# Addressing the V product's weight slices through TensorE registers loaded from a table

## The reference

```
src_trans = jnp.einsum('bsf,of->bso', src, W_src) + b_src      # src: (8, 512, 512), W_src: (512, 512)
src_key, src_val = jnp.split(src_trans, 2, axis=2)             # K: outputs 0 to 255, V: outputs 256 to 511
...
attn = jax.nn.softmax(scores, axis=-1)
tgt_update = jnp.einsum('bhts,bshd->bthd', attn, v)
```

## Time and profile before

| | |
|---|---|
| time, median of 2 runs | 1054.62 us (1053.51 to 1055.73) |
| time of the profiled execution | 1049.61 us |
| its span, first to last instruction | 1047.5 us |
| PE busy | 1003.0 us (96%) |
| PEld busy | 761.4 us (73%) |
| DVE, ACT, POOL busy | 655.4, 467.2, 389.4 us |
| mean granted TensorE clock | 0.989 of full speed |

### The profile page before, as it was taken

How to read it: one execution, slowest core, us unless ns; L and a number is a source line. 1 busy time by engine, 2 the same in 40 slices (tenths; PEclk the granted TensorE clock), 3 DMA queues, 4 the chain that set the end, 5 groups by cost and what they waited for, 6 DMA issues and landing times.

```text
span 1047.5 us, 14744 instructions
## 1 busy us (share of the span) xinstructions
PE 1003.0 (96%) x5070; PEld 761.4 (73%) x5070; DVE 655.4 (63%) x1510; ACT 467.2 (45%) x881; POOL 389.4 (37%) x355
## 2 busy tenths in 40 slices
PE   4889999999999998899999999999999999999998
PEld 3656767676767664567888888888888888888886
DVE  6866767776767577445665566556556556555544
ACT  3447565666565646445424333333333333333322
POOL 2569797879797967345310010010010100100000
PEclk9999999999999997999999999999999999999999
DMA  7543342424242223325333232242341232332230
GB/s 232 131 132 93 101 132 67 128 72 134 70 114 70 65 64 101 81 81 122 95 72 68 52 81 58 54 82 50 63 80 42 71 82 46 74 75 60 67 72 24
DMA packets 84377, 87.87 MB, mean 84 GB/s; under 512 B 13160, under 2 KB 66296, under 8 KB 84304
## 3 DMA queue, kind: packets, MB, share of 16 engines
q1 hardware_dynamic: 82384, 84.85, 32.9%
q10 hardware_dynamic: 1920, 2.10, 0.6%
HBM read 56.99 MB, written 4.46 MB: 59 GB/s over the span
## 4 chain that ended last, share of the span: by engine, by line
PE 89%; DVE 5%; ACT 2%; SPq 1%; issue 1%; POOL 1%; DMA 1%; DVEq 0%; ACTq 0%; POOLq 0%
PE ps L659 49%; PE pst L659 18%; PE ps L765 5%; PE ps L738 5%; PE pst L754 5%; PE ps L665 4%; DVE mx L1196 1%; PE ps L778 1%; SPq L611 1%; SPq L546 1%; ACT e_buf L866 1%; DVE lg L1277 1%; ACT ctx_h L866 0%; DVE wsrc_l L1145 0%; DMA x<-in_x 0%
## 5 line engine op out<-in xcount | busy, mean ns | idle before, releaser
L659 PE MATMUL ps<-x_h,weights 128*128 128x512 f32 x1088 | 365.6, 397 | 2.8 <-DVE sg L1297 2.0
L659 PEld LDWEIGHTS ps<-x_h,weights 128*128 128x128 f32 x1088 | 204.4, 188 | 52.7 <-issue 2.5
L1196 DVE TENSOR_REDUCE mx<-ps 128x1 f32<-128x512 f32 x256 | 173.2, 684 | 95.4 <-PE ps L738 94.8
L659 PE MATMUL ps<-x_l,weights 128*128 128x512 f32 x544 | 214.5, 394 | 0.0
L866 ACT ACTIVATE hh<-qb 128x512 fp32r<-128x512 f32 x136 | 86.0, 632 | 287.7 <-DVE qb L1311 268.2
L659 PE MATMUL pst<-hh,weights 128*128 128x512 f32 x544 | 193.2, 397 | 0.0
L866 ACT ACTIVATE e_buf<-pst 128x512 f32<-128x512 f32 x256 | 147.1, 595 | 100.4 <-PE pst L754 90.5
L1300 DVE TENSOR_TENSOR qb<-ps,sg 128x512 f32<-128x512 f32 x136 | 94.0, 691 | 135.9 <-PE ps L659 132.2
L1316 DVE TENSOR_TENSOR hl<-qb,hh 128x512 fp32r<-128x512 f32 x136 | 94.3, 693 | 92.2 <-ACT hh L866 92.0
L1406 POOL TENSOR_TENSOR e_sums<-e_sums,e_buf 128x1024 f32<-128x1024 f32 x60 | 143.4, 2390 | 8.6 <-ACT e_buf L866 2.5
L1358 POOL TENSOR_SCALAR ve<-mv 128x4 f32<-128x4 f32 x8 | 1.8, 229 | 337.8 <-DVE mv L1238 337.8
(11 more groups left out here) (154 smaller groups left out, 1360.7 us busy)
## 6 DMA issues: line engine op xcount, KB each, us to landing
cb<-combine_scratch SPq DMA_DIRECT2D x128, 256.0 KB, 4.7
q_stack<-q_h SPq DMA_DIRECT2D x128, 64.0 KB, 2.0
k_stack<-k_h SPq DMA_DIRECT2D x124, 64.0 KB, 2.0
ctx_raw<-in_ctxT SPq DMA_DIRECT2D x7, 1024.0 KB, 5.3
q_stack<-q_l SPq DMA_DIRECT2D x64, 64.0 KB, 2.0
out_x<-ob SPq DMA_DIRECT2D x16, 256.0 KB, 2.1
k_stack<-k_l SPq DMA_DIRECT2D x62, 64.0 KB, 2.0
x<-in_x SPq DMA_DIRECT2D x7, 512.0 KB, 6.8
```

What stands on the lines that cost most here:

```text
L659: ins = engine.matmul(dst, lhsT, rhs, start=start and n == 0, stop=stop and n == len(terms) - 1)
L1196: engine.tensor_reduce(MX[:, g % 2, h // 2, h % 2, q:q + 1], bank(step), AX.X, ALU.max).then_inc(sem("max"), 1)
```

## The change

GpSimd writes the numbers 0, 1, 2, 3 into a tile `KT` of one partition (`k_table`) at the start. In TensorE's program each step (half 0, n 0) of `v` loads the four numbers into registers, and all four `v` steps of the batch address the slice `k` of the moving operands `WSh` and `WSl` through them. The values loaded are the constants that stood there before, so every matmul reads the same bytes as before.

```
+        KT = s1("k_table", [1, 4], I32)
...
+            k_values = []
...
                     tok = tok_of(half, n)
-                    ins = mms(ps[:, 256 * n:256 * n + 256],
-                              [(l, r) for k in range(4) for r, l in
-                               hi3(WSh[:, k, 256:512], WSl[:, k, 256:512], CH[:, k, tok], CL[:, k, tok])])
+                    pe.wait_ge(sem("k_table"), 1)
+                    if half == 0 and n == 0:
+                        k_values = [engine.value_load(KT[0:1, k:k + 1], min_val=0, max_val=3) for k in range(4)]
+                    terms = []
+                    for k in range(4):
+                        at_k = bass.ds(k_values[k], 1)
+                        wh = WSh[:, at_k, 256:512].rearrange("p a o -> p (a o)")
+                        wl = WSl[:, at_k, 256:512].rearrange("p a o -> p (a o)")
+                        terms += [(l, r) for r, l in hi3(wh, wl, CH[:, k, tok], CL[:, k, tok])]
+                    ins = mms(ps[:, 256 * n:256 * n + 256], terms)
...
                     engine.memset(ON[:, :], 1.0).then_inc(sem("ones"), 1)
+                    engine.iota(KT[:, :], pattern=[[1, 4]], base=0, channel_multiplier=0).then_inc(sem("k_table"), 1)
```

## The result

The changed kernel takes 1067.7 us (median of 2 runs, 1067.50 to 1067.89) against 1054.62: a ratio of 1.0138 with a 95% interval of 1.0103 to 1.0173. Five more rounds beside the kernel before gave 1066.76 against 1053.30, a ratio of 1.0124 (1.0103 to 1.0146). So it is 1.2 to 1.4% slower, some 13 us. Executions to which the chip granted a much lower clock are left out of all ratios: one of 1648.9 us at 0.559, in the first run of the late six places, whose trace is not read either, and one of 1120.8 us at 0.846 with loads in the expert stage. I had expected 1079, 2.3% slower, in a range of 1056 to 1110: right in direction and place, too large by a factor of nearly two.

The account below looks back on a forecast made before the run. PE was taken as the bound; batch 0's 3.0, batch 1's 0.5, six stalls' 12.5 and the clock's 8.8 summed to 24.8 us, which on 1054.6 gave about 1079 us, 2.3% slower, range 1056 to 1110.

Parts of the forecast that it names:

- What bounds the kernel, and where the change bites: PE, busy 1003.0 of 1047.5 us; idle time would appear ahead of each batch's first V matmuls, not the other V steps.
- The lead: Ahead of the first V step in batches 1 to 7, the sequencer runs 0.97 us ahead of PE; none at batch 0.
- The hold: At each of eight places, four loads (2.52 us) and nine small instructions (0.53) hold the sequencer for 3.05 us.
- rival 1: At the loads, no change: loads cheap or lead longer, 0.77 us held at 0.06 a load, time 1055.4; chance 0.23.
- The stall: Ahead of the first V matmuls of batches 2 to 7, PE loses 2.1 us each, 12.5 us in all.
- The clock: Behind the stalls of batches 2 to 7, TensorE drops to half clock, costing 1.46 us each, 8.8 us in all.
- rival 4: Behind the stalls the clock stays up: sum 16.0 us, time 1070.6; counted within the likeliest case's lower half, no separate chance.
- Batch 0 and batch 1: First two V places: 3.0 us at batch 0; 2.1 at batch 1, of which 0.5 is left after ACT's idle time.
- The matmuls with register addresses: In all V steps, 384 matmuls keep their durations and their 0.118 us spacing: nothing added.
- The small instructions among the matmuls: Seven standing among V matmuls at each place, at most 0.4 us a place, 3.4 in all; put at nothing.
- The likeliest case: At the eight places, loads of 0.4 to 0.9 us with or without the clock drop, 1064 to 1090 us; chance 0.38.
- the signs of being wrong: Idle time of the predicted size elsewhere than ahead of first V matmuls, or a changed length of the expert stage.

Follow-up runs that it names:

- the late six places: Loads and register addresses only in batches 2 to 7, against the kernel before: ratio 1.0104, then 1.0067 in a second run.
- loads in the expert stage: The kernel before plus four unused loads ahead of one expert unit of each batch, constant V addresses: ratio 0.9983 to the kernel before.
- the kernel with loads only: The changed kernel with its 32 loads kept but constant addresses in all V matmuls: ratio 1.0105 to the kernel before.
- eight loads: The changed kernel with eight loads a place in place of four, the last four used: ratio 1.0458 to the kernel before.
- load-once kernel: The changed kernel with the four loads at batch 0 only, registers used in all batches: ratio 1.0022 to the kernel before.

## Why the prediction was right or wrong

**What bounds the kernel, and where the change bites: right.** PE is the bound, its busy time hardly changes, and the loss stands as idle time without a semaphore ahead of the first V matmul of each batch and at no other V step.

**The lead: right.** 0.97 us was read from the earlier trace rows; 0.92 was measured at the same place. The assumption under it, that the sequencer does not pass a waiting matmul, was argued then and is shown now: the loads start 0.05 us behind the maxima in the changed kernel, and behind the exponentials with the loads one matmul earlier.

**The hold: near, and partly by luck.** 3.05 us against 2.74. The load itself was half of what I took from an issue of a DMA, 0.30 in place of 0.63, while the two instructions behind it with their gaps took 0.27 where I had 0.12, and the gap behind the load took 0.07. The two errors go against each other. The argument for 0.59, that every instruction in the trace that goes to memory takes as long, was misread too: of the 702 issues of DMAs in the trace of before 212 took less than 0.55, the shortest 0.36. The Trainium skill's floor of about 600 ns for a `tensor_load` ("DMA: Bandwidth & Descriptors", "Latency and other measured facts") is not what this trace shows for a value in SBUF; its 200 ns per register ("Runtime: NRT & Kernel Launch", "Instruction fetch mechanics") is nearer to the 0.30 of this trace, yet rival 1, which it spoke for, did not come: with checks and gaps a load holds the sequencer for 0.64.

**The stall: 2.1 against 1.57.** 0.3 of the difference is the hold. The other 0.23 is a term that I left out: the weight load is normally hidden under the previous matmul, and behind a stall PE wins that time back. Six places: 12.5 predicted, 9.4 measured.

**The clock: wrong, and the largest error.** 8.8 us were in the sum and none came in batches 2 to 7. The step that failed is "a stall of 2.1 us is on the wrong side": I took the length of a single idle time to decide, with a boundary between 1.34 us and 1.59 us, and put my own estimate above it. The idle times came out at 1.25 to 1.48, and the clock stayed at 1.00 behind all six, in both traces of the changed kernel. But the boundary doesn't hold. The trace of before has an idle time of 2.05 us with the clock up behind it, which I had overlooked:

```profile
452.61 0.48 PE L659 MATMUL ps<-x_h,weights 128*128 128x512 f32 x1 [2.05 <-DVE sg L1297]
452.60:456.00 3.40, 3.39 (x15) 1.00 0.13 33
```

In the kernel with loads only, 1.76 us at batch 0 left it up:

```profile
24.18 0.38 PE L660 MATMUL ps<-wsrc_h,ctx_h 128*128 128x256 f32 x1 [1.76 <-issue]
24.10:27.00 2.90, 2.82 (x23) 1.00 0.84 199
```

In the changed kernel the wait of the earlier trace rows, as long as before, stands ahead of a stretch at 0.50, as does the stall at batch 0:

```profile
46.01 0.47 PE L747 MATMUL ps<-k_stack,q_stack 97*128 97x512 f32 x1 [1.35 <-DVE mx L1205]
46.80:53.60 6.80, 6.80 (x18) 0.50 0.42 101
26.30:29.70 3.40, 3.40 (x19) 0.50 0.72 171
```

So one idle time between about 1.3 and 2.1 us was followed by either level, and what decides there besides its length stays open. Whether stalls of 2.1 us would have brought the clock down is not shown. The price itself was of the right size: eight loads, with 4 us of idle time, lost 1.5 us and more at each place. A term as uncertain as this should have been a case with a chance of its own. As rival 4 it stood there, with 1070.6 us, and that is where the time fell: 16.0 us predicted, 13.1 to 13.5 measured.

**Batch 0 and batch 1: the stalls right, what follows them not.** 3.0 us at batch 0 stands against an idle time of 2.72 (2.26 in the second trace, 2.89 with the load-once kernel). But the clock falls to 0.50 behind it in all three, which cost 1.5 us more, 0.4 of it absorbed by a later wait, and for which the sum had nothing, although it counted such a term for shorter stalls. At batch 1 the stall of 1.6 us is followed by the loss of ACT's idle time of 1.59 as foretold: PE's shift goes up by 1.58 and down again by 1.62. The half-speed stretch of before behind it, which I took to stay, doesn't come in the changed kernel's traces, and PE gains 1.6 us by it; the kernel with loads in the expert stage, which has none here, lacks it too, so the change isn't shown to be the cause.

**The matmuls with register addresses, and `IOTA`: right at nothing.** The first is shown by the load-once kernel. `IOTA` starts at 1.4 us and takes 126 ns, long before the first load at 22.7. The small instructions among the matmuls, put at nothing, show nothing either: the 0.1 us behind a stall is there in the kernel with loads only, too.

The time without the clock term would have been 1070.6, and with the 0.23 us it would have been 1069. The hold of 2.74 in place of 3.05 takes off 2 us more, which comes to 1067; that batches 0 and 1 don't disturb this is luck, since their errors have opposite signs and the start differs by 3 us between executions.

**The chances.** The likeliest case (1064 to 1090) holds the time. But 0.57 stood on more than 2% slower and 0.42 on less, and it is the less that came. None of the signs of being wrong came: at no other place is there idle time of this size that the change is shown to cause, and the expert stage changes its length by 0.05 us in the first trace and 1.5 in the second, which has one stretch at half clock more there. The stretches at 0.50 that were to stand behind each stall came at batch 0 alone.

## What to carry to other kernels

A register load costs the engine nothing as long as the sequencer's lead covers it: look for what releases the last wait ahead of the place and compare that time with the engine's own start. The lead depends on the place (here 0.9 us ahead of the V steps and 3.6 us at the two other places where it was measured, one in attention and one in the expert stage); put loads behind a long run of matmuls and ahead of a wait, and load once what does not change. State the bounds of a value at the load, so that its check is made once, and give a fall of the clock that was read off one or two idle times a case of its own: the same wait can be followed by either level in the next execution.

## What the runs showed of the hardware

- A load of one 32-bit value from SBUF into a register of TensorE's sequencer took 0.295 to 0.306 us at batch 2, 0.50 for the first of the program, and up to 0.51 for single others in the kernel with eight loads. With the arithmetic (0.146 to 0.151) and the check (0.018) behind it and the gaps between them, one load holds the sequencer for 0.64 us; without them the loads start 0.37 us apart (109.8 to 110.9 for four).
- Behind a matmul that waited for a semaphore, the first load started 0.04 to 0.05 us after the releasing engine's work had ended, at 7 of 7 places in each of two kernels: the sequencer did not pass the waiting matmul.
- A matmul whose moving operand is addressed by a register was handed over at the same pace as others: 0.118 us apart, 282 ns median.
- An address computation of 55 to 60 ns and one register instruction more for three matmuls left these 0.12 us apart, but six register instructions for three matmuls did not: 0.76 us a slice in place of 0.36.
- Idle times of PE of 1.25 to 1.48 us ahead of the V steps of batches 2 to 7 left the clock at 1.00 in both traces of the changed kernel, and those of 3.9 to 4.3 us brought it to 0.50 at 6 of 6 places. In between a single idle time does not decide: 1.76 and 2.05 us were followed by 1.00, and 1.35, 1.59 and 2.09 us by 0.50.
